# Count rounds of a graph kernel that send on values before they are normalized, with the heavy rows prepared earlier

## The reference

```python
# layer 3: three rounds with weighted edges
res = 0.1 * y; out = y
for _ in range(3):
    agg = segment_sum(norm[:, None] * out[row], col)
    out = clip(agg * 0.9 + res, 0.0, 1.0)
x = x + out
h = maximum(_layernorm(x), 0.0)
# layer 4: three rounds with edge counts, and a self edge for every node
src, dst, wn = _gcn_norm(edge_index, n)          # wn = dinv[src] * dinv[dst]
z = h
for i in range(3):
    z = segment_sum(wn[:, None] * z[src], dst)
    z = relu(z)
    mean = jnp.mean(z, axis=0); var = jnp.mean(square(z - mean), axis=0)
    z = (z - mean) * rsqrt(var + 1e-5) * gammas[i] + betas[i]
x = x + z
```

## Time and profile before

| | |
|---|---|
| median of three runs | 3460.56 us |
| the profiled execution, span from first to last instruction | 3465.3 us |
| PE busy | 2974.6 us (86%) |
| DVE busy | 2742.9 us (79%) |
| mean DMA rate over the span | 112 GB/s |
| weighted rounds 1 and 2, with their ends | 3147 to 3316 us |
| count rounds, to the last DVE instruction | 3316 to 3462 us |

### The profile page before, as it was taken

One profiled execution on the slowest core, in us unless ns is written; L12 is line 12 of the kernel. 1 busy time (PEld: TensorE's weight loads), 2 busy tenths in 40 slices (PEclk: granted clock), 3 DMA queues, 4 the chain that ended last, 5 costly groups with the idle time before them and its releaser, 6 DMA issues. The chain is left out here.

```text
span 3465.3 us, 69301 instructions
## 1 busy us (share of the span) xinstructions
PE 2974.6 (86%) x19703; PEld 2370.4 (68%) x19703; DVE 2742.9 (79%) x6018; ACT 2280.7 (66%) x3192; POOL 2141.3 (62%) x1629
## 2 busy tenths in 40 slices
PE   3888788988856999999999999999999976657657
PEld 3677677777745888888888888888888851113257
DVE  6678988888856999999999999999999973441065
ACT  3678688888836888888888888888888842220000
POOL 4048888888877777777777777777777730000000
PEclk9899899999977999999999999999999997798778
DMA  9943222222222333333333333333333359998940
GB/s 400 419 154 38 12 15 15 15 16 16 15 25 41 53 53 52 50 53 51 50 53 51 50 53 51 51 53 52 50 53 52 50 187 426 426 391 342 373 172 6
DMA packets 265695, 388.67 MB, mean 112 GB/s; under 512 B 149903, under 2 KB 200838, under 8 KB 259254
## 3 DMA queue, kind: packets, MB, share of 16 engines
q0 software_dynamic: 149184, 120.78, 20.7%
q1 hardware_dynamic: 100034, 195.42, 16.6%
q10 hardware_dynamic: 16416, 71.74, 5.1%
HBM read 260.01 MB, written 127.78 MB: 112 GB/s over the span
## 5 line engine op out<-in xcount | busy, mean ns | idle before, releaser
L585 POOL DMA_INDIRECT both<-kept x782 | 1333.0, 1705 | 439.8 <-issue 194.6
L923 PEld LDWEIGHTS ps<-prod,big 128*128 128x128 f32 x7840 | 1133.9, 190 | 137.7 <-DVE prod L1290 133.0
L923 PE MATMUL ps<-prod,big 128*128 128x170 f32 x7840 | 1183.2, 310 | 22.5 <-DVE prod L1290 17.4
L593 POOL DMA_INDIRECT kept<-feat_dram,kept x782 | 760.8, 973 | 243.2 <-issue 233.1
L668 ACT ACTIVATE big<-iota_b,kept 128x640 f32<-128x640 f32 x1029 | 779.0, 815 | 13.6
L914 PE MATMUL ps<-prod,onehot 128*128 128x320 f32 x3920 | 684.5, 325 | 81.2 <-DVE prod L1320 79.6
L914 PEld LDWEIGHTS ps<-prod,onehot 128*128 128x128 f32 x3920 | 597.7, 194 | 112.9 <-DVE prod L1320 84.5
L673 ACT ACTIVATE big<-big 128x2560 f32<-128x2560 f32 x196 | 458.0, 2337 | 277.2 <-PE ps L923 277.1
L988 PE MATMUL ps<-w2mix,kept 65*128 65x384 f32 x1568 | 559.3, 500 | 21.7 <-ACT kept L720 20.4
L1462 DVE TENSOR_REDUCE kept<-kept 128x80 f32<-128x1280 f32 x392 | 561.4, 1471 | 0.0
L988 PEld LDWEIGHTS ps<-w2mix,kept 65*128 65x128 f32 x1568 | 284.2, 191 | 179.7 <-issue 25.5
(11 more groups left out here) (235 smaller groups left out, 3028.9 us busy)
## 6 DMA issues: line engine op xcount, KB each, us to landing
both<-big POOLq DMA_DIRECT2D x40, 1910.0 KB, 91.2
big<-both SPq DMA_DIRECT2D x24, 1600.0 KB, 11.8
big<-both SPq DMA_DIRECT2D x24, 1528.0 KB, 13.2
kept<-keys_dram SPq DMA_DIRECT2D x196, 128.0 KB, 3.0
kept<-in_wT SPq DMA_DIRECT2D x196, 128.0 KB
adj_c<-kept ACTq DMA_DIRECT2D x42, 400.0 KB, 31.6
kept<-adj_c SPq DMA_DIRECT2D x9, 1600.0 KB, 22.4
adj_w<-kept ACTq DMA_DIRECT2D x16, 800.0 KB, 33.6
```

What stands on the lines that cost most here:

```text
L585: pool.indirect_dma_start(both, bass.IndirectOffsetOnAxis(ap=sc_idx[:, c:c + 1], axis=0), sc_val[:, c // 2, c % 2, :], None, compute_op=AL ...
L593: pool.indirect_dma_start(gath[:, s % 2, k, :], None, feat_dram, bass.IndirectOffsetOnAxis(ap=src_i[:, 4 * s + k:4 * s + k + 1], axis=0)). ...
L923: mm = pe.matmul(part_sums(part, MSG), onehot[:, q, k, part * P:(part + 1) * P], prod[:, q, k, 0:HI * MSG], start=False, stop=False, skip_ ...
```

## The change

It has three parts.

**Values not normalized.** A count round no longer sends normalized values. The evacuation of bank `b` makes the next round's three bf16 parts right away from relu(z) (`of_bank`, `clipped`, `in_parts`), and the batch norm's scale and shift are applied in the evacuation of the next round. As propagation is linear, `sum(wn * (s*z + t))` is `s * sum(wn * z) + t * reach`, with `reach` the sum of `wn` over a node's edges; round 3 gets it from three more columns (99 for 96, `dparts` holds the parts of `dinv`). The sums for mean and variance are made while PE is in bank 0 and 1 of the next round, and PE's two small matmuls for them stand in bank 1 and behind it. Rounds 4 and 5 run bank by bank from their first block. The parts of round 4 lie in another buffer (`znarrow`) than those of rounds 3 and 5 (`zwide`).

**Heavy part earlier.** `find_slots` stands in round 1 behind group 0, `find_rows` in thirds (`PICK_SETS`) behind groups 1 to 3. The overflow part comes in 17 pieces of 184 columns; DVE converts 4 in round 1, 8 in round 2 and 5 in round 3. As `big` is in use then, GpSimd stores each piece to DRAM (`over_dram`), and SP loads the whole at the end (800 KB). PE wants it in round 3 in bank 1 after source block 12, and each bank is signalled when it is done.

**The last batch norm** uses sums over banks 0 to 3 taken about a provisional mean while PE is still in bank 4; `x` gets its shift in that time too.

The core of the diff:

```diff
-EIGHTH = TCOLS // 8
+PIECES = 17
+PIECE = TCOLS // PIECES
+PIECES_BY_ROUND = (0, 4, 12, PIECES)
+PICK_SETS = ((0, 12), (12, 24), (24, NA))
-EARLY = 13
+EARLY = 8
+MOST = NA - BANK_D
@@ sync
+                    sp.wait_ge(s_overpad, 16)
+                    for q in range(2):
+                        sp.wait_ge(s_overout[q], 16 * len(range(q, PIECES, 2)))
+                    sp.dma_start(over16, over_dram).then_inc(s_over16, 16)
@@ gpsimd
-            for e in range(8):
-                if e >= 2:
-                    pool.wait_ge(s_over, e - 1)
-                pool.indirect_dma_start(over_in[:, e % 2, :], None, eighths,
...
+            for e in range(PIECES + 1):
+                if e < PIECES:
+                    if e >= 2:
+                        pool.wait_ge(s_over, e - 1)
+                    pool.indirect_dma_start(over_in[e % 2], None, pieces,
...
+                if e >= 1:
+                    pool.wait_ge(s_over, e)
+                    pool.dma_start(over_dram[:, (e - 1) * PIECE:e * PIECE],
+                                   over_out[:, (e - 1) % 2, :]).then_inc(s_overout[(e - 1) % 2], 16)
@@ tensor, weighted rounds
                 for k in range(GROUPS - 1):
                     group(k, (3 * k, 3 * k + 1, 3 * k + 2))
+                    if r == 1 and k == 0:
+                        find_slots()
+                    elif r == 1 and k <= len(PICK_SETS):
+                        find_rows(k - 1)
@@ tensor, count rounds
+                if opening:
+                    for s in range(EARLY):
...
                 for b in range(BANKS):
+                    mine = range(b * BANK_D, (b + 1) * BANK_D)
+                    for s in range(EARLY if opening else 0, NA):
+                        if b == 0 and not opening and s % BANK_D == 0:
+                            pe.wait_ge(s_z, 7 + BANKS * (r - 4) + s // BANK_D)
+                        add_block(s, mine)
+                        if b == 0 and not opening and s == MOST - 1:
+                            heavy_z(0, MOST)
+                        if b == 1 and s == 12:
+                            if not opening:
+                                feature_sums(2 * r - 7, 0)
+                            add_over(0)
+                        if b == 4 and s == 13 and r == 5:
+                            feature_sums(5, 0)
...
+                    if b == 1 and not opening:
+                        feature_sums(2 * r - 6, 1)
@@ vector, weighted rounds
+                    heavy_rows()
+                if r >= 1:
+                    heavy_pieces(PIECES_BY_ROUND[r - 1], PIECES_BY_ROUND[r])
                 copy_sums(r)
@@ vector, count rounds
+            def heavy_pieces(e0, e1):
+                for e in range(e0, e1):
+                    dve.wait_ge(s_overin[e % 2], 16 * (e // 2 + 1))
...
+                    if e >= 2:
+                        dve.wait_ge(s_overout[e % 2], 16 * (e // 2))
+                    V.tensor_copy(over_out[:, e % 2, :], whole).then_inc(s_over, 1)
...
+            for b in range(BANKS):
+                dve.wait_ge(s_acc, b + 1)
+                of_bank(b, False)
+                clipped(b, False)
+                in_parts(znarrow, b * BANK_D, (b + 1) * BANK_D)
+            for r in range(4, 6):
+                sum_of(0, h[:, :, :]).then_inc(s_fs, 1)
+                spread(r - 1)
+                dve.wait_ge(s_acc, BANKS * (r - 3) + 1)
+                of_bank(0, True)
+                coefficients(r - 1)
+                for b in range(BANKS):
+                    if b:
+                        dve.wait_ge(s_acc, BANKS * (r - 3) + b + 1)
+                        of_bank(b, True)
+                    clipped(b, True)
+                    if r == 4:
+                        in_parts(zwide, b * BANK_D, (b + 1) * BANK_D)
...
```

More of the change, by code:

```diff
@@ L1077, in add_over @@
                                        skip_group_check=True)
                     mm.then_inc(s_acc, 1)
-                for s in range(EARLY):
-                    for i, (a0, a1) in enumerate(SPLITS):
-                        if s == a0:
-                            pe.wait_ge(s_z, r * 3 - 5 + i)
-                    add_block(s, range(NA))
-                    if opening and s == 7:
-                        find_rows()
-                pe.wait_ge(s_z, r * 3 - 3)
-                for a in range(NA):
-                    mm = pe.matmul(ps[:, 5, 0:3 * FEAT], picks[:, a, :], parts(a), start=(a == 0), stop=(a == NA - 1))
@@ L1103, in count_round, with heavy_z @@
-                for i in range(2):
-                    pe.wait_ge(s_fs, r * 2 - 6 + i + 1)
-                    pe.matmul(ps[:, 7, i * FEAT:(i + 1) * FEAT], ones_f[:, :], fsum[:, 0, :],
+                def heavy_z(a0, a1):
+                    for a in range(a0, a1):
+                        mm = pe.matmul(ps[:, 5, 0:width], picks[:, a, :], parts(a), start=(a == 0), stop=(a == NA - 1),
+                                       skip_group_check=True)
+                    if a1 == NA:
+                        mm.then_inc(s_zc, 1)
@@ new lines, in feature_sums @@
+                def feature_sums(n, i):
+                    pe.wait_ge(s_fs, n)
+                    pe.matmul(ps[:, 7, i * FEAT:(i + 1) * FEAT], ones_f[:, :], fsum[:, 0, :],
+                              start=True, stop=True).then_inc(s_fsp, 1)
+                if opening:
+                    for s in range(EARLY):
+                        if s in (0, 5):
+                            pe.wait_ge(s_z, 4 + s // 5)
+                        add_block(s, range(NA))
+                    pe.wait_ge(s_z, 6)
@@ L1134, in _ @@
             spmm_round(1)
-            find_slots()
             spmm_round(2)
-            count_round(3, True)
-            with pe.Fori(4, 6) as r:
-                count_round(r, False)
+            for r in range(3, 6):
+                count_round(r)
         @block.vector
@@ new lines, in clipped @@
+            def clipped(b, scaled):
+                mine = slice(b * BANK_D, (b + 1) * BANK_D)
+                if scaled:
+                    shift = squares[0][:, mine, :] if b < BANKS - 1 else squares[1]
+                    link(V.tensor_tensor(h[:, mine, :], h[:, mine, :],
+                                         fsum[:, 4, :].unsqueeze(1).broadcast_to([P, BANK_D, FEAT]), ALU.mult))
+                    link(V.tensor_tensor(h[:, mine, :], h[:, mine, :], shift, ALU.add))
+                link(V.scalar_tensor_tensor(out=h[:, mine, :], in0=h[:, mine, :], scalar=0.0,
+                                            in1=dinv[:, 1, mine].unsqueeze(2).broadcast_to([P, BANK_D, FEAT]),
+                                            op0=ALU.max, op1=ALU.mult))
```

270 lines of the change are left out of this document (167 added, 103 removed).

## The result

The changed kernel takes 3490.11 us (median of 4 runs, 3485.82 to 3491.21), beside 3459.31 us before: the ratio is 1.009, 95% interval 1.0073 to 1.0106. It is slower by about 31 us, where 12 us less were forecast. The profiled execution has a span of 3484.1 us, 18.8 more than before. It is the fastest of its four and before's was one of the slower, so the pair of profiles shows 12 us less of a loss than the medians do. Four executions far longer than the others of their kernel are in no ratio of this document: 8018.84 us (e1), 3660.94 (e2), 4438.46 (g3) and 6296.73 (the kernel before, beside f4 to f6 and g2).

A forecast was written before the change was run, and what follows sets the result against it. The prediction took full DMA engines to bound the weighted rounds, and PE and DVE in turns the count rounds. -29.4 + 10 + 7 + 0.5 = -12 us on a 3465.3 us span gave 3453.3, median 3448.5, range 3434 to 3464.

The forecast's parts named there:

- Every rival: Three: moved bytes nearly free (3438.5 us, chance 0.12), a wash (3459.5, 0.19), gathers queue under load (3471.5, 0.11).
- The weighted rounds: Rounds ahead of the count rounds: bytes of 14 gathers and 12 stores lengthen them while DMA is full, +7 us.
- rival 3: Weighted rounds: gathers queue under load and the rounds wait for them, +11 us, time 3471.5; chance 0.11.
- The opening round: Count round 3: PE waits 15.4 us in bank 1 for `over16`, which comes over DRAM; costs 10 us.
- T: End of PE's last overflow matmul in round 3: 3356.9 us before, forecast 3366.9 after.
- The rounds behind it: From T to the last output pass: DVE and PE overlap, 75.6 us for 105.0, a gain of 29.4 us.
- the sign to look for: Profile after, behind the overflow matmuls: two PE waits of 1 to 2 us a round in bank 1.
- The small passes: Five small DVE passes behind `dinv`, around 2830 us: at most 1.6 us, taken as +0.5.

The follow-up runs named there:

- e1: The changed kernel with the SBUF addresses of the kernel before, its grown and new tensors placed behind `big`; ratio 1.0053.
- e2: The kernel before with the SBUF layout of the changed kernel and no instruction added; ratio 1.0002.
- g3: The changed kernel with only the engine starting the 17 stores of pieces changed, ScalarE in place of GpSimd; 3459.37 us, ratio 0.9988.
- f4: The kernel before with 18 unused 16 KB stores at the end of GpSimd's queue; ratio 1.0096.
- f5: The kernel before with 9 unused gathers at the end of GpSimd's queue; ratio 1.0.
- f6: The kernel before with 27 small memsets at the end of GpSimd's queue; ratio 0.9981.
- g2: The changed kernel with all pieces made before round 3 and their stores started by ScalarE; 3442.87 us, ratio 0.9947.
- h4: The kernel before with one unused 16 KB store as the last instruction of GpSimd's queue; ratio 1.0108.
- The 13 kernels named above: e2, e3, f1 to f6 and h1 to h5: experiments whose last layer does the kernel before's work; edge layers' end to span end 639.3 to 647.1 us.
- f1: The kernel before with 9 unused gathers and 18 unused 16 KB stores at the end of GpSimd's queue; ratio 1.0077.
- h1: The kernel before with 6 unused 16 KB stores at the end of GpSimd's queue; ratio 1.0066.
- h2: The kernel before with 18 unused stores of one partition (128 bytes) each at the end of GpSimd's queue; ratio 1.0051.
- h3: The kernel before with 18 unused loads from DRAM at the end of GpSimd's queue, each waiting for the one before; ratio 1.0076.
- e3: The kernel before with the DRAM tensor `over_dram` and one store to it, behind the edge work and ahead of the gathers of heavy rows; ratio 0.9996.
- f2: The kernel before with PE's loop over count rounds 4 and 5 written out; ratio 0.9974.
- f3: The kernel before with 86 small memsets added on DVE in weighted round 2; ratio 0.999.
- h5: The kernel before with six unused 16 KB stores at the start of GpSimd's queue, behind the stores of zeros; ratio 1.0008.

## Why the prediction was wrong

**The step that failed** is in the first sentence: "the windows of the last 320 us, the only part that the change touches but for five small DVE passes". The diff touches instructions only there, but the new stores at the end of GpSimd's queue go with 32.3 us in the edge layers, over 2 ms ahead of them. Every rival shared the assumption, and the sum put the edge layers at nothing without a word. Its size is outside the range because nothing in the sum stood for it: 3453.3 + 32.3 = 3485.6 for the span, measured 3484.1. That plain DMAs at the end of that queue are the cause is shown from both sides: one put into the kernel before makes the loss (h4), and with all 17 taken to ScalarE's queue it goes (g3).

**The weighted rounds**: +7 forecast, 8.2 measured. The 13 kernels named above, whose rounds 1 and 2 do before's work, take 160.0 to 163.7 us from the turn of round 0 to that of round 2, before 162.7, and e1, with after's rounds, costs 6.6 over before, so the agreement is good to 2 or 3 us. The gathers landed in 7.4 us at the median beside the full engines, so rival 3, which needed 11, did not come, and the PSUM copies were released by PE. (The gather at which rival 3 turns the sign is 16.8 us by its own formula, 2 x (16.8 + 2.2) - 26 = 12, and not 17.5.) The DMA share fell to 0.99 at 391 GB/s, so part of the 8.2 may be rate and not bytes; no run separates them.

**The opening round**: +10 forecast. From the first cast of the parts it was 3316.45 to 3356.91 and is 3356.69 to 3404.22: +7.1. PE waited 10.9 us for `over16` and not 15.4. Counted from the first cast, the last piece was stored at 26.1 us (27.9 forecast), the load took 4.09 us (5.4 forecast), and PE was there at 19.5 (17.9 forecast). Each of the three shortens the wait, and the first two shorten the round.

The prediction misread one row here. 3356.91 is the end of the five overflow matmuls of bank 0, behind which DVE starts, and not of the last. A timeline of before, from 3356 us on, has all 25:

```profile
3356.34 2.16 PE L1076 MATMUL ps<-zc,big 128*128 128x96 bf16 x25 [8.05 <-DVE big L1580]
```

They end at 3358.5. With T as the prediction defines it the opening round costs 5.5 us (8.4 forecast) and the rounds behind it give 27.0 (27.8 forecast). The sum of the two is the same either way.

**The rounds behind it**: -29.4 forecast, -28.6 measured (105.0 to 76.4 us). T to the last output pass was put at 75.6. PE's waits for feature sums in bank 1 are two of 1.5 us in all, one in each of rounds 4 and 5, for 1.7 each; the sign to look for, two a round, was written wrongly, as the working has one.

**The small passes**: +0.5 forecast; the rest between the end of the edge layers and the first cast, without rounds 1 and 2, is -0.3.

The errors of the terms are small and of both signs (+1.2, -2.9, +0.8, -0.8), and with a spread of some 8 us in this stretch among equal kernels it is in part luck that 12 and 13.5 lie so close.

Rival 3 had the sign of the result, but its mechanism is not what happened.

## What to carry to other kernels

Check every stage's start time before explaining a stage: here one row of an untouched step, 32.3 us late, says that the loss is elsewhere. Where an untouched stage is paced by GpSimd's indirect DMAs, compare how many of them it issues in a fixed window, and look at what was added to that engine's queue, behind them too. Here the change could be had without the loss by starting its 17 small stores from another engine's queue: 1.009 became 0.9988 by that alone, and 0.9947 with the pieces earlier. Moving only the last of them was not run.

## What the runs showed of the hardware

One plain DMA behind everything else on GpSimd's queue goes with longer issues of its scatter-adds from 200 us on, by 17 to 35 us at the first feature gather; where nothing else was changed (f1, f4, h1 to h4) the ratio is 1.005 to 1.011. How a later instruction reaches back so far is open. It is not the SBUF or DRAM layout (e1 to e3), not the number of instructions (f2, f3, f6), of DMAs (f5, h5) or of bytes (h2).

The issues do not get longer evenly: they come in levels. Of the adds between 300 and 985 us 157 of 318 take 1.56 us or less before and 90 of 306 after; the commonest of the longer ones take about 1.9, 2.0, 2.4 to 2.5 and 2.65 us. Around 600 us of the kernel before, GpSimd's and DVE's timelines, rows of each (start us, us, what):

```profile
598.07 1.54 POOL L585 DMA_INDIRECT both<-kept  x1 [0.30 <-issue]
...
601.82 1.78 POOL L585 DMA_INDIRECT both<-kept  x1 [0.30 <-issue]
...
608.38 2.65 POOL L585 DMA_INDIRECT both<-kept  x1 [0.30 <-issue]
```

```profile
598.35 1.49 DVE L1320 TENSOR_TENSOR prod<-kept 128x1280 fp32r<-128x1280 f32 x1
...
602.11 1.78 DVE L1311 TENSOR_SCALAR onehot<-iota_b,kept 128x640 fp32r<-128x640 f32 x3
...
606.12 1.76 DVE L1311 TENSOR_SCALAR onehot<-iota_b,kept 128x640 fp32r<-128x640 f32 x3
...
608.13 1.49 DVE L1320 TENSOR_TENSOR prod<-kept 128x1280 fp32r<-128x1280 f32 x1
...
611.26 1.06 DVE L1311 TENSOR_SCALAR onehot<-iota_b,kept 128x640 fp32r<-128x640 f32 x2
```

The issue beside a TENSOR_TENSOR at 598 us takes 1.54 us; the one beside TENSOR_SCALAR passes at 602 us takes 1.78. But the longest, 2.65 us from 608.38 to 611.03, lies between two groups of TENSOR_SCALAR passes, beside a TENSOR_TENSOR of the same form as the first. The Trainium skill, "SBUF — State Buffer", Who interferes with whom, says that DVE and GpSimd share a port pair, that TENSOR_SCALAR can take it for a whole instruction and that the other then waits, so that a DMA started by GpSimd waits for its descriptors. The first two issues agree with it, and so do the one-hot passes, longer by 5% (593 to 623 ns) in the kernel whose adds are longer; their mean is 602 to 624 ns in all nine slow kernels and 588 to 597 in the others. The third issue does not agree, and neither do the adds as a whole: by the timelines those between 300 and 985 us that overlap a TENSOR_SCALAR pass of over 0.3 us last 1.80 us in the mean before, and those that overlap none 1.82 (1.94 and 1.87 after). That the last DMA shifts how the two engines' instructions meet (the shortest issue is 1541 to 1543 ns in all nine slow kernels, 1538 or 1539 in the others) would fit, but it was only argued and no run shows it.
